# Rounding the weights of a quantized feed-forward layer on GpSimd by an added constant

## The reference

```python
wb = w.reshape(O, I // 32, 32)
s = maximum(max(abs(wb), axis=-1, keepdims=True) / 7, 1e-12)
wq = clip(round(wb / s), -8, 7) * s
```

## Time and profile before

| | |
|---|---|
| median of 3 runs | 1537.63 us (1537.39 to 1537.69) |
| profiled execution | 1535.16 us, span 1533.4 us |
| busy share of the span | TensorE 95%, VectorE 57%, ScalarE 48%, GpSimd 33% |
| mean granted TensorE clock | 0.996 |

### The profile page before, as it was taken

The page is one execution under the profiler, slowest core; times in us unless marked ns, Lnnn a source line. Parts: engine busy times, 40 slices in busy tenths (PEclk is TensorE's granted clock), DMA queues, the critical chain, the costliest instruction groups (busy, mean ns, idle before and its releaser), DMA issues.

```text
span 1533.4 us, 32957 instructions
## 1 busy us (share of the span) xinstructions
PE 1450.5 (95%) x12566; PEld 1122.4 (73%) x12566; DVE 880.5 (57%) x1909; ACT 732.6 (48%) x1799; POOL 507.2 (33%) x701
## 2 busy tenths in 40 slices
PE   6999998997999999999997999999999999999998
PEld 5877776446877777777775677488858876885887
DVE  5988898499546666666666788543234224323322
ACT  5887777398535455545553787322121212221211
POOL 2444552001036965976666888100000000000000
PEclk9999999999999999999999999999999999999999
DMA  8000000007131262146210000124404431441230
GB/s 307 22 7 3 1 1 22 0 0 212 36 137 57 55 240 82 48 164 233 55 48 1 2 1 2 49 96 144 145 14 144 145 109 49 144 153 53 97 144 14
DMA packets 60520, 124.13 MB, mean 81 GB/s; under 512 B 5008, under 2 KB 15760, under 8 KB 57872
## 3 DMA queue, kind: packets, MB, share of 16 engines
q1 hardware_dynamic: 60432, 122.94, 23.2%
HBM read 108.24 MB, written 14.68 MB: 80 GB/s over the span
## 4 chain that ended last, share of the span: by engine, by line
PE 69%; DVE 12%; POOL 9%; issue 5%; ACT 3%; DVEq 0%; DMA 0%; SPq 0%; POOLq 0%; ACTq 0%
PE ps L975 24%; PE ps L556 15%; PE ps L778 5%; PE ps L562 4%; PE ps L772 4%; PE ps L1026 4%; PE ps L798 3%; POOL R L2068 2%; PE ps L750 2%; DVE R L1743 2%; POOL R L2050 2%; PE ps L809 2%; DVE amax L1610 1%; POOL R L2042 1%; PE ps L657 1%
## 5 line engine op out<-in xcount | busy, mean ns | idle before, releaser
L975 PE MATMUL ps<-R 128*128 128x256 f32 x1792 | 388.6, 379 | 3.4 <-DVE R L1892 3.4
L975 PEld LDWEIGHTS ps<-R 128*128 128x128 f32 x1792 | 340.0, 190 | 52.2 <-issue 6.5
L556 PE MATMUL ps<-R 128*128 128x128 f32 (+1 forms) x1344 | 305.2, 386 | 1.8 <-ACT R L1090 0.9
L556 PEld LDWEIGHTS ps<-R 128*128 128x128 f32 x1344 | 189.7, 194 | 109.8 <-issue 104.6
L1298 ACT ACTIVATE R<-ps,c_nmx 128x257 f32<-128x257 f32 x256 | 118.1, 474 | 126.4 <-DVE c_nmx L1767 126.4
L2050 POOL TENSOR_TENSOR R<-R,c_inv 128x1024 f32<-128x1024 f32 x64 | 121.0, 1891 | 127.1 <-DVE c_inv L1778 127.1
L1743 DVE COPY R<-ps 128x512 f32<-128x512 f32 x128 | 88.2, 689 | 81.4 <-PE ps L798 80.0
L778 PE MATMUL ps<-x_wv,R 128*128 128x256 f32 x512 | 121.1, 379 | 0.0
L2139 POOL TENSOR_SCALAR g_ve<-g_mv 128x4 f32<-128x4 f32 x4 | 0.9, 236 | 331.1 <-DVE g_mv L1841 331.1
L778 PEld LDWEIGHTS ps<-x_wv,R 128*128 128x128 f32 x512 | 92.5, 190 | 10.1
L1370 ACT ACTIVATE R<-R,ffn_s 128x256 f32<-128x256 f32 x32 | 16.2, 508 | 167.5 <-DVE R L1899 167.5
(11 more groups left out here) (223 smaller groups left out, 2518.7 us busy)
## 6 DMA issues: line engine op xcount, KB each, us to landing
R<-quadrant_sums SPq DMA_DIRECT2D x32, 1024.0 KB, 6.8
R<-in_f_hq SPq DMA_DIRECT2D x32, 768.0 KB, 4.4
R<-in_ctxT SPq DMA_DIRECT2D x64, 257.0 KB, 2.7
R<-in_f_hq SPq DMA_DIRECT2D x8, 1024.0 KB, 8.7
quadrant_sums<-R SPq DMA_DIRECT2D x8, 1024.0 KB, 8.1
R<-in_ctxT SPq DMA_DIRECT2D x16, 256.0 KB, 3.8
k_ahead<-R SPq DMA_DIRECT2D x16, 256.0 KB, 3.6
R<-k_ahead SPq DMA_DIRECT2D x16, 256.0 KB, 3.1
```

The lines of the kernel that those rows point to most:

```text
L556: r = mm(dst, w[:, ki, fo * P:(fo + 1) * P], src[:, ki, :], start=(ki == 0), stop=(ki == KI - 1))
L975: r = mm(ps[:, 4 * (g % 2) + bk, half * HALF:(half + 1) * HALF], f_wr[g % 3][:, w, ki * P:(ki + 1) * P], src[:, k, ki, :], start=(ki == 0) ...
```

## The change

The divide on VectorE now writes its quotient in f32 in place. A new step on GpSimd, `b_w_round`, adds the constant 12582912 (1.5 x 2^23) to it in place, which leaves the integer in the low bits of the f32 sum. The last step on VectorE subtracts the constant again and multiplies by the scale in one instruction. The weight steps move: `d_w_scale` from slot 6 to 4, `d_w_inverse` from 11 to 6, `d_w_divide` from 12 to 8, where it follows `d_turn_values` of its lane. `d_w_multiply` stays at 17. `b_w_round` stands at slot 19 of GpSimd's list. The integer buffer goes.

```diff
-        w_int = [view(WT + 192 * m, 192).bitcast(I16).rearrange("p (a b) -> p a b", b=32) for m in range(3)]
...
-                    v.tensor_tensor(w_int[m][:, :, :], w, wi.broadcast_to(W_PART), ALU.mult).then_inc(w_rounded, 1)
+                    v.tensor_tensor(w, w, wi.broadcast_to(W_PART), ALU.mult).then_inc(w_divided, 1)
...
                     dve.wait_ge(w_rounded, 3 * i + m + 1)
-                    v.tensor_tensor(w, w_int[m][:, :, :], ws.broadcast_to(W_PART), ALU.mult).then_inc(wT_quant, 1)
+                    v.scalar_tensor_tensor(w, w, -MAGIC, ws.broadcast_to(W_PART), ALU.add, ALU.mult)\
+                        .then_inc(wT_quant, 1)
...
-                attention(A0, [(0, d_norm), (2, d_w_max), (6, d_w_scale), (8, d_turn_values), (9, d_mask),
-                               (9, d_max), (9, d_shift), (11, d_w_inverse), (12, d_sums), (12, d_w_divide),
+                attention(A0, [(0, d_norm), (2, d_w_max), (4, d_w_scale), (6, d_w_inverse), (8, d_turn_values),
+                               (8, d_w_divide), (9, d_mask), (9, d_max), (9, d_shift), (12, d_sums),
...
+            def b_w_round(kind, m, i):
+
+                if m < 3:
+                    w = w_part(m, i)[0]
+                    pool.wait_ge(w_divided, 3 * i + m + 1)
+                    p.tensor_tensor(w, w, magic[:, :].unsqueeze(2).broadcast_to(W_PART), ALU.add).then_inc(w_rounded, 1)
+
...
-                attention(A0, [(8, b_rsqrt), (12, b_bias), (17, b_keys)])])
+                attention(A0, [(8, b_rsqrt), (12, b_bias), (17, b_keys), (19, b_w_round)])])
```

More of the change, by code:

```diff
@@ L309, in link @@
             eng.wait_ge(chain, links[chain])
-        w_max, w_scale, w_inverse, w_rounded = map(sem, ("w_max", "w_scale", "w_inverse", "w_rounded"))
+        w_max, w_scale, w_inverse, w_divided, w_rounded = map(
+            sem, ("w_max", "w_scale", "w_inverse", "w_divided", "w_rounded"))
         wT_quant, wT_turned, wT_copied = sem("wT_quant"), sem("wT_turned"), sem("wT_copied")
@@ L409, in key_rows, with w_part @@
             return bank[l][1][j * L:(j + 1) * L, :].rearrange("p (c k) -> p c k", k=L)
+        def w_part(m, i):
+            return [a.rearrange("p (i b) c -> p i b c", i=NT)[:, i] for a in
+                    (w_nat[m], wmax[:, m], wsc[:, m], winv[:, m])]
         def halves(ap):
@@ L1505, in d_add @@
                     .then_inc(s["x_updated"], 1)
-            def w_part(m, i):
-                return [a.rearrange("p (i b) c -> p i b c", i=NT)[:, i] for a in
-                        (w_nat[m], wmax[:, m], wsc[:, m], winv[:, m])]
             def d_w_max(kind, m, i, n):
```

## The result

| | before | changed |
|---|---|---|
| median of 8 runs | 1537.51 us (1535.22 to 1540.17) | 1541.62 us (1539.20 to 1545.57) |
| profiled execution | 1535.16 us, span 1533.4 us | 1539.20 us, span 1537.4 us |

The changed kernel takes 1.0026 times the time of the one before (95% interval 1.0014 to 1.0037), 4.1 us more by the medians, and 2.2 to 5.7 by that interval. The forecast was 1542.0, and 4.4 us more.

The account below looks back on a forecast made before the run. TensorE holds 69% of the chain; in stage `A0` GpSimd's keys are on it or within 0.15 us. Twelve intervals +3.6 us, first lane 2 interval +0.3, tail +0.5: +4.4 on 1537.63 gives 1542.0 us, range 1536.5 to 1545.5.

Parts of the forecast that it names:

- The bare chain: Stage `A0`: norm to keys' end 3.72 us, to mask 0.92, to next norm 2.80; no interval falls below 7.49 us.
- The round: `b_w_round` on GpSimd, between rsqrt and keys: 0.88 us added to each interval of lanes 2, 3 and 0.
- Intervals: Twelve in stage `A0`: lanes 2 and 0 8.44 us, lane 3 8.37, lane 1 8.01; 99.78 against 96.19, +3.6.
- The first lane 2 interval: Before the twelve intervals, in the first round: keys end at 131.21, mask starts at 132.13 instead of 131.81, +0.3 us.
- The tail: After the twelve intervals: last lane 3 interval pays 0.88 us less a slack of 0.36, +0.5 us.
- The divide: `d_w_divide` on VectorE: waits for GpSimd's bias in lane 1, 0.45 us lost; hidden by 0.24 us in lanes 2 and 3.
- The scale's 0.07 us: `d_w_scale` between subtraction of the maximum and next norm, on the chain in lanes 0, 1 and 2: 0.07 us each.
- the prediction's caution about the clock: Head of the next stage: granted clock 0.96 over 40 us, 1.6 us of time, which may fall otherwise.
- the round would be hidden: Rival: with 0.88 us of slack behind the keys every interval falls to 7.49; -6.3 us, 1531.3; chance 0.10.
- Cancelling: Rival: `b_w_round` at 0.73 us, lane 1 divide ahead of the bias, scale free; +0.7, 1538.3 us; chance 0.20.
- The divide stalled twice: Rival: bias goes ahead of the divide in lanes 2 and 3, 0.5 us in seven intervals; 1545.5 us; chance 0.08.

Follow-up runs that it names:

- The second addition: Changed kernel with a second GpSimd addition of the same size ahead of `b_w_round`, its result unread; 1550.76 us against 1537.24 for the kernel before.
- the round's removal from there: Changed kernel with `b_w_round` at slot 18 instead of 19, 1537.60 us, or at 17 directly behind the keys, 1533.53; kernel before 1537.24.
- the kernel with the scale off the chain: Changed kernel with `b_w_round` at slot 17 behind the keys and `d_w_scale` back at slot 6; 1530.57 us against 1537.05 for the kernel before.
- the old slots: Changed kernel with VectorE's weight steps at their slots from before, `b_w_round` still at 19; 1561.61 us against 1537.05 for the kernel before.

## Why the prediction was right

**The bare chain.** The chain norm, rsqrt, keys, scores, mask, norm was said to pace the intervals, and no slack behind the keys to hide a round. The second addition, which lengthened the intervals of lanes 0, 2 and 3, and the round's removal from there, which shortened them, show it from both sides. Its length was taken as 7.49 us for every lane. With nothing in its way, in the kernel with the scale off the chain, it is 7.6 in lanes 3 and 0 and 7.4 in lanes 1 and 2. So the terms of the sum err with both signs, and the total is nearer than its worst term.

**The round.** Forecast 0.88 us, measured 0.825. The estimate of 0.97 us that stands beside the forecast is too high: the round is 1.67 times as long as the free divide's 0.495 us. It stands where the list said, and the keys end 4.66 us after the norm in lane 3 (forecast 4.6).

**Intervals.** Lane 3: forecast 8.37, measured 8.40. Lane 0: 8.44 and 8.53. Lane 1: 8.01 and 8.00. Lane 2: 8.44 and 8.20, the term that was most off. The bare chain that I took for it came from lane 1, where the multiply stands beside GpSimd's small instruction and lengthens it to 0.46 us; in lane 2 there is no multiply, and it takes 0.21. Twelve intervals were to rise by 3.6 us and rose by 3.19. The three rows are lane 1's multiply and small instruction, and lane 2's small instruction:

```profile
217.62 0.50 DVE L1540 SCALAR_TENSOR_TENSOR R<-R,wsc 128x384 f32<-128x384 f32 x1
217.72 0.46 POOL L1954 TENSOR_SCALAR nmr<-mv 128x1 f32<-128x1 f32 x1
...
225.66 0.21 POOL L1954 TENSOR_SCALAR nmr<-mv 128x1 f32<-128x1 f32 x1
```

**The ends.** The first lane 2 interval was to gain 0.3 and went from 7.81 to 8.05. The tail was to gain 0.5: from the last norm to the last residual addition it went from 20.55 (230.62 to 251.17) to 20.95 (233.11 to 254.06), 0.4. From the lane 1 norm at 118.55 (after: 117.53) to that addition, the stage grew by 136.53 - 132.62 = 3.9 us; I had 4.4. This is the closer test of the forecast: that the medians differ by 4.1 is a nearer hit than their interval, 2.2 to 5.7 us, can vouch for.

**The divide.** It was to be stalled by the bias in lane 1 for 0.45 us and be hidden in lanes 2 and 3; the rows above show the delay in lane 1 (0.45 us) and, for lane 3, an end 0.42 us after the keys and a mask 0.91 after them, within 0.01 us of what was forecast. The scale's 0.07 us on the chain is seen in the timeline of the kernel with the scale moved back; that its old place also spares GpSimd's small instruction was not foreseen.

**Outside the stage.** The two profiled executions differ by 4.0 us as well, but partly by chance, in terms that cancel. The changed one reached that lane 1 norm 1.0 us earlier, the stage took 3.9 more, and all that follows its last residual addition 1.15 more (1283.35 and 1282.20). Before, the clock fell as TensorE began the weights' transposes; after, it was full there, but fell twice later, where the context is projected for layer 1 (line 892) and under the down projection (line 754), and before it was full in the window of the latter:

```profile
251.80:255.30 3.50, 3.45 (x18) 3.48 (x19) 3.15 (x11) 2.48 (x5) 1.28 (x2) 0.55 0.00 0
```

```profile
372.00:376.00 4.00, 4.00 (x12) 3.21 (x12) 3.96 (x3) 4.00 (x4) 0.00 (x0) 0.60 0.78 218
```

```profile
394.00:398.00 4.00, 3.54 (x11) 3.00 (x12) 1.92 (x5) 4.00 (x8) 0.00 (x0) 0.71 0.11 43
```

The first row is from the kernel before, the other two from the changed one. The first lies over most of the 24 transposes, which took 4.31 us before and 2.81 after. So the prediction's caution about the clock in the earlier trace rows was in place, with either sign. It may be part of why eight runs of one kernel spread over 5.0 and 6.4 us: of the changed kernel's runs, the one of 1539.20 us had a clock of 0.995, the one of 1545.57 us 0.991. Only one execution of each kernel was profiled.

**The rivals.** That the round would be hidden fell with the 8.7 us of waits for the keys. Cancelling fell too: the round came 0.055 us below the value taken, not 0.15, the stall in lane 1 was real, and the moved scale cost its 0.07. The divide stalled twice was not seen: in lane 3 it went ahead of the bias.

## What to carry to other kernels

What work costs on an engine that is half idle depends on where it stands in that engine's order. The twelve additions cost 0.01 us over twelve intervals in one place and 4.6 us in another. Look for the instruction behind it, and ask how long after its last input something waits for it; here one slot of 20 was worth 4 us (1541.6 to 1537.6), and the next one another 4 (1533.5), that one because it puts the divide ahead of the bias.

When an instruction takes 0.5 to 2.1 us for the same shape, find what ran on the other engine before moving the work away. Here the cure was to order the two engines, by a wait that does no work. With it and the moved steps the kernel was 5 us faster than before, integers kept, and its intervals were as short as with the rounding moved.

Measure such a change by the period of its pipeline in the trace: the intervals of two kernels agreed to 0.01 us over 95, where medians of a dozen runs leave about 1.5 us open either way. But the period is not the time: 1.4 us won in the intervals did not appear in the medians of two kernels.

## What was not expected of the hardware

Where TensorE waited most, its granted clock was lower. Over the twelve intervals it was 1.00 in the changed kernel, with 8.7 us of waits for the keys in the stage; 0.94 with the second addition, where these waits were 14.8 us; and 0.95 with the old slots, where they were 25.0 us. In all the other kernels it was 1.00 there. So part of the loss of these two may be the clock's; how much is not separated. The falls themselves are no mark of these kernels: each of the nine profiled executions has several, each a few microseconds long, at other places. In the kernel before they lie at 250 to 256, 828 to 832 and 844 to 850 us. After the stage's last residual addition the nine took 1282.2 to 1286.9 us for the same work, so the falls can hide a gain of 1.5 us in one execution.

An instruction on GpSimd of 0.21 us takes 0.46 beside a VectorE multiply of 0.5 us that began first, and the 2 us divides of the kernel before were the same thing with the roles exchanged. The Trainium skill ("SBUF — State Buffer", "Who interferes with whom") says that a VectorE instruction with two SBUF inputs contends with a GpSimd one that reads SBUF, and that the order of issue decides which of them blocks. The traces agree in both directions: the divide took 0.52 us free and up to 2.11 where GpSimd's instruction had begun first, and the small GpSimd instruction took 0.46 where the multiply had.
